# Each expert's weights read once and split in place by GpSimd, in a gated attention and mixture-of-experts block on Trainium2

## The reference

```
x = x + tanh(g_xattn) * attention(layernorm(x), keys and values from ctx and from x)   # wq, wk, wv, wo 512x512
n = layernorm(x)
shared = silu(n @ W1s.T) * (n @ W3s.T) @ W2s.T                  # 704 hidden channels
probs = softmax(n @ Wg.T); each token takes its 4 best of 16 experts, with their probs as weights
routed = sum over the 4 of  weight * (silu(n @ W1[e].T) * (n @ W3[e].T)) @ W2[e].T      # 352 hidden channels
out = x + tanh(g_ffn) * (shared + routed)
```

## Time and profile before

| what | us |
|---|---|
| timed runs, median (3 runs) | 1185.95 |
| timed runs, lowest and highest | 1185.82, 1188.97 |
| profiled execution, its own time | 1180.43 |
| its span, first to last instruction | 1178.5 |
| busy in the span: PE, PEld | 1087.8, 915.3 |
| busy in the span: DVE, ACT, POOL | 535.3, 276.4, 510.7 |
| GpSimd's subtractions of expert weights (144) | 181.6 |
| HBM read, written | 182.49 MB, 58.72 MB |

### The profile page before, as it was taken

One profiled execution on the slowest core, in us unless ns is written; L12 is line 12 of the kernel. 1 busy time (PEld: TensorE's weight loads), 2 busy tenths in 40 slices (PEclk: granted clock), 3 DMA queues, 4 the chain that ended last, 5 costly groups with the idle time before them and its releaser, 6 DMA issues. The chain is left out here.

```text
span 1178.5 us, 19426 instructions
## 1 busy us (share of the span) xinstructions
PE 1087.8 (92%) x5378; PEld 915.3 (78%) x5379; DVE 535.3 (45%) x944; ACT 276.4 (23%) x576; POOL 510.7 (43%) x632
## 2 busy tenths in 40 slices
PE   3999999999999959898979999999899999979997
PEld 3888778878878727676878888898898988967775
DVE  2243463445336257864333333334334333336846
ACT  1231132122113011111223333233233333331110
POOL 4720201202200246020666575567757775628752
PEclk9999999999999969899989999999999999988998
DMA  9411320311211446147978889887898999866775
GB/s 343 192 72 72 129 87 3 139 71 71 107 71 34 189 155 224 45 153 223 341 266 273 306 293 317 279 285 272 319 311 286 322 313 316 274 188 220 241 240 158
DMA packets 109825, 241.68 MB, mean 205 GB/s; under 512 B 13216, under 2 KB 52128, under 8 KB 101600
## 3 DMA queue, kind: packets, MB, share of 16 engines
q0 software_dynamic: 21504, 123.48, 29.6%
q1 hardware_dynamic: 77920, 98.89, 25.1%
q10 hardware_dynamic: 10368, 18.88, 4.4%
HBM read 182.49 MB, written 58.72 MB: 205 GB/s over the span
## 5 line engine op out<-in xcount | busy, mean ns | idle before, releaser
L989 POOL TENSOR_TENSOR expert_lo<-expert_raw,expert_hi (+1 forms) x144 | 181.6, 1295 | 54.5 <-DMA expert_raw<-we_rest 42.7
L88 PE MATMUL c_ps_u<-expert_hi,xT_hi 128*128 x576 | 193.1, 335 | 4.0 <-DVE xT_lo L1520 4.0
L88 PE MATMUL c_ps_u<-expert_hi,xT_lo 128*128 x576 | 186.4, 324 | 0.0
L88 PE MATMUL c_ps_u<-expert_lo,xT_hi 128*128 x576 | 185.8, 322 | 0.0
L88 PE MATMUL c_ps_y<-expert_hi,hT_hi 128*128 (+1 forms) x216 | 88.8, 411 | 29.1 <-DVE hT_lo L1525 29.1
L88 PEld LDWEIGHTS c_ps_u<-expert_hi,xT_hi 128*128 128x128 f32 x576 | 109.0, 189 | 5.6 <-issue 4.6
L88 PEld LDWEIGHTS c_ps_u<-expert_lo,xT_hi 128*128 128x128 f32 x576 | 109.6, 190 | 0.0
L88 PEld LDWEIGHTS c_ps_u<-expert_hi,xT_lo 128*128 128x128 f32 x576 | 109.0, 189 | 0.0
L1515 DVE STREAM_TRANSPOSE xT<-xs 128x512 f32<-128x512 f32 x73 | 51.5, 706 | 88.9 <-DMA xs<-bounce_dram 87.2
L88 PE MATMUL c_ps_y<-expert_hi,hT_lo 128*128 (+1 forms) x216 | 88.1, 408 | 0.0
L88 PE MATMUL c_ps_y<-expert_lo,hT_hi 128*128 (+1 forms) x216 | 88.0, 407 | 0.0
(11 more groups left out here) (263 smaller groups left out, 2356.7 us busy)
## 6 DMA issues: line engine op xcount, KB each, us to landing
expert_hi<-we POOLq DMA_DIRECT2D x16, 1920.0 KB, 8.1
expert_raw<-we POOLq DMA_DIRECT2D x14, 1920.0 KB, 13.1
xs<-bounce_dram SPq DMA_DIRECT2D x304, 64.0 KB, 2.3
y_dram<-y ACTq DMA_DIRECT2D x72, 256.0 KB, 3.9
bounce_dram<-xg SPq DMA_DIRECT2D x72, 256.0 KB, 2.8
ctxT_hi<-ctxT POOLq DMA_DIRECT2D x4, 1024.0 KB, 7.5
ctxT_raw<-ctxT SPq DMA_DIRECT2D x4, 1024.0 KB, 5.7
ctx_raw<-ctx SPq DMA_DIRECT2D x4, 1024.0 KB, 4.9
```

The costliest lines, as they stand in the source:

```text
L88: last = pe.matmul(out, a[i], b[j], start=(n == 0), stop=(n == 3 * len(pairs) - 1))
L989: last = eng.tensor_tensor(lo, raw, hi, ALU.subtract)
```

## The change

GpSimd's loads of the high part go away everywhere (expert 0, expert 1, and in each round). Each expert is loaded once, raw. `split_expert` first copies the raw weights into `w_hi`, in nine pieces of up to 512 columns, so that the copy rounds them to float32r; it waits for its own last copy on a semaphore (`hi_made`), runs a small instruction (`hold`), and then makes the nine subtractions as before, in place. The load of expert 1's raw part moves from SyncE, ahead of the stores of the sums, to GpSimd, behind a wait for all eight stores of gathered tiles. The wait for `second_raw_in` ahead of GpSimd's first step goes, since `w_in` counts that load now. The way of the tiles through DRAM stays.

```diff
-def split_expert(eng, later, base, sem, width=W13 + W2):
+def split_expert(nc, keep, eng, later, base, expert, sem):
 
-    pieces = [(P, at, min(width, W13 + W2 - at)) for at in range(0, W13 + W2, width)]
-    for rows, start, n in pieces + [(FT, W13 + W2, D)]:
+    made = keep["hi_made"]
+    pieces = [(P, at, min(D, W13 + W2 - at)) for at in range(0, W13 + W2, D)] + [(FT, W13 + W2, D)]
+    for rows, start, n in pieces:
+        hi, raw = (part(w, rows, base, start, n) for w in (later.w_hi, later.w_raw))
+        last = eng.tensor_copy(hi, raw)
+    last.then_inc(made, 1)
+    eng.wait_ge(made, expert + 1)
+    hold(nc, eng, keep, 6)
+    for rows, start, n in pieces:
         hi, lo, raw = (part(w, rows, base, start, n) for w in (later.w_hi, later.w_lo, later.w_raw))
         last = eng.tensor_tensor(lo, raw, hi, ALU.subtract)
     last.then_inc(sem, 1)
...
@@ routing_phase, SyncE
-            for v in range(QUAD):
-                sp.wait_ge(keep["bounced"][v], 32)
-            load_expert(sp, later.w_raw, WE, io, 1, keep["second_raw_in"])
...
@@ routing_phase, GpSimd
-            load_expert(pool, later.w_hi, 0, io, 0, hi_in["first"])
             pool.wait_ge(hi_in["down"], 32)
             pool.wait_ge(raw_in["down"], 32)
             split_down(pool, later.d_hi, later.d_lo, later.d_raw, True, down_ready)
-            pool.wait_ge(hi_in["first"], 32)
             pool.wait_ge(raw_in["first"], 32)
-            split_expert(pool, later, 0, first_ready, D)
+            split_expert(nc, keep, pool, later, 0, 0, first_ready)
...
             pool.wait_ge(sh.t_free, 2 * IT)
             pool.wait_ge(scheduled, 1)
-            load_expert(pool, later.w_hi, WE, io, 1, keep["w_in"])
+            for v in range(QUAD):
+                pool.wait_ge(keep["bounced"][v], 32)
+            load_expert(pool, later.w_raw, WE, io, 1, keep["w_in"])
...
@@ expert_phase, GpSimd
-                load_expert(pool, later.w_hi, base, io, e, w_in)
                 load_expert(pool, later.w_raw, base, io, e, w_in)
...
-                    pool.wait_ge(w_in, e * 64 + 32)
-                    split_expert(pool, later, base, w_ready, D)
+                    pool.wait_ge(w_in, e * 32 + 32)
+                    split_expert(nc, keep, pool, later, base, e + 1, w_ready)
...
-            pool.wait_ge(keep["second_raw_in"], 32)
```

More of the change, by code:

```diff
@@ L1057, in routing_phase @@
         raw_in = {k: sem(k + "_raw_in") for k in ("down", "first")}
-        hi_in = {k: sem(k + "_hi_in") for k in ("down", "first")}
+        hi_in = {"down": sem("down_hi_in")}
         down_ready = sem("down_ready")
@@ L1724, in program @@
         keep["y_out"], keep["base_out"] = [sem(f"y_out{v}") for v in range(QUAD)], [sem(f"base_out{u}") for u in range(2)]
-        keep["w_in"], keep["second_raw_in"] = sem("w_in"), sem("second_raw_in")
+        keep["w_in"], keep["hi_made"] = sem("w_in"), sem("hi_made")
         keep["last_down_in"], keep["last_xs_in"] = sem("last_down_in"), [sem(f"last_xs{i}_in") for i in range(IT)]
```

## The result

| what | before | after |
|---|---|---|
| timed runs, median, us | 1185.88 | 1228.47 |
| timed runs, lowest and highest, us | 1180.12, 1188.97 | 1227.21, 1233.23 |
| span of the profiled execution, us | 1178.5 | 1226.2 |
| HBM read, MB | 182.49 | 147.88 |

The ratio is 1.0372, with a 95% interval of 1.0324 to 1.0421. The change makes the kernel 3.7% slower. The forecast was 1178.3, in a range of 1168 to 1206, so both the sign and the range were wrong.

What follows compares the result with a forecast made beforehand. The prediction took GpSimd's round for each expert to set the expert stage's pace. Start -5.0, five-tile rounds -6.0, four-tile rounds -2.4 and end +5.75 summed to -7.7 us: 1178.3 against a median of 1185.95, range 1168 to 1206.

Steps and rivals of the forecast that it cites:

- Copies, hold and wait: In each split on GpSimd: nine copies 5.4 us, small held instruction 0.2, wait some 0.1, together 5.75 a round.
- The cast's slope: GpSimd's one-input cast, 0.857 ns a column, used to price a copy of 512 columns at 0.63 us.
- The rival of a dearer copy: Copies above 0.69 us make GpSimd's round longer; about 0.77 gives 1196 (chance 0.16), dearer still or no shorter queue 0.12.
- The shorter queue: GpSimd's load queue without high-part loads: first gather stored 9.7 us after the split's end, not 16.2, so 6.5 less.
- It doesn't do what it says: Rival: bytes don't hold the first gather, its wait stays near 16, rounds grow 5.75: 1267 us; within a shared 0.12.
- Raw weights: In four-tile rounds the raw weights land about 9.4 us after the split's end, ending GpSimd's wait of 6.28.
- Rounds: GpSimd's rounds: eight five-tile ones -0.75 us each to 33, six four-tile ones about -0.4 each to 26.3.
- Start and end: First split at 562.3, 5 us earlier; after the last split nothing leaves the queue, so its copies add 5.75.
- Added: nine copies ahead of the subtractions: Step pricing the new copies, hold and wait in each GpSimd split at 5.75 us, bounds 4.8 to 11.4.
- a copy of 1.03 us: Case of the dearer copy at twice the affine select's time for 256 columns: 51 us more, 1229.

Runs made afterwards that it cites:

- The moved kernel after: The changed kernel with 120 already fulfilled waits ahead of GpSimd's expert loop, which move the loop to 510 to 808 in the list: 1173.18 us, ratio 0.9913.
- 569 to 915: The moved kernel after with the nine copies, a wait and a hold made a second time in each split: 1313.02 us, ratio 1.1096.
- 580 to 878: The changed kernel with 260 already fulfilled waits ahead of GpSimd's loop instead of 120, the same work otherwise: 1233.9 us, ratio 1.0441.

## Why the prediction was wrong

The moved kernel after is the change without the refetching, and the sum can be read against it. It ran at 8.2 us below before (forecast 7.7 below, 1178.3 in all; measured 1173.18 beside 1181.34). That the two numbers lie so near is partly luck: in the two profiled executions, from which the terms below are read, the span is 4.2 shorter (1174.3 against 1178.5), and the terms come to that.

- *Copies, hold and wait.* Forecast 0.63 a copy and 5.75 a round. In the moved kernel nine copies took 5.34 in some rounds and 4.87 in the others, that is 0.63 or 0.57 for each of 8.5 widths; from the first copy to the first subtraction it was 5.57 (664.46 to 670.03) and 5.09 (691.08 to 696.17). A whole split grew from 11.4 to 17.0 in the mean of the fifteen, 5.6. Made twice the copies cost 5.7 to 5.8. The cast's slope was the right row. The rival of a dearer copy, the Trainium skill's body of 768 ns ("GPSIMD Engine Reference", section 3.1) among it, didn't come.
- *The shorter queue.* Forecast 6.5 less, a store 9.7 after the split's end. Measured 10.2 in the moved kernel, 10.4 in after: 6.0 less, the lower of the two values (6.0 and 7.1) between which 6.5 was taken. "It doesn't do what it says" is out.
- *Raw weights.* Forecast in at 9.4. In the moved kernel the load is issued at 681.77 and the next split starts at 691.08, still 1.40 idle for `we_rest`:

```profile
681.77 0.60 POOL L980 DMA_DIRECT2D expert_raw<-we  x1
...
691.08 1.18 POOL L990 CAST expert_hi<-expert_raw  x2 [1.40 <-DMA expert_raw<-we_rest]
```

  That is 9.3 after the issue. The wait of some 6 us is gone, down to the register work that I had put at 1.3.
- *Rounds.* Forecast 33.0 and 26.3; measured 33.5 in the mean of five-tile rounds, with 36.0 for the first and 33.1 for the other seven, and 26.6 for four-tile ones. From the first split to the last it is 427.7, against 431.6: -4.0, where I had -8.4. The mis-sized terms are the queue (6.0, not 6.5) and the first round, which I had at -0.75 like the others and which grew by 2.1 (567.27 to 601.15 before): there GpSimd stands 1.86 and 2.26 for "issue" where it first comes to the loop's code (0.24 and 1.00 before).
- *Start and end.* First split forecast 562.3, measured 562.21 (5.1 earlier). Last split at 989.86 against 998.88, 9.0 earlier, and the span 4.2 shorter, so the end lost 4.8 (forecast 5.75).

**The step that failed** is in "Added: nine copies ahead of the subtractions", and in the rivals. It costs an added instruction by its duration alone, and so puts the fetching of GpSimd's code at nothing without giving a reason. The change also adds 20 instructions to GpSimd's loop of four tiles, and 29 ahead of it (421 to 450 where it starts, 278 to 298 in length). By that the loop came to lie over four pieces of code, and at each of the 16 jumps back between its 17 passes (the first four tiles are written out ahead of it) GpSimd fetched code again: 80 packets more, five for each jump. DMA traffic of the kernel after between 654 and 1070 us, in which it jumps back 14 times:

```profile
q14 instruction: 70, 0.57, 0.4%
```

The moved kernel has one packet in the same stretch. The fetching costs 55.3 us (1228.47 less 1173.18; 50.8 when each is set against before on its own chip), seven times the net gain that I had added up. None of my rivals had it: 1229 stands in the text, but for a copy of 1.03 us, so the number is there by chance and its mechanism isn't.

Why one fetch costs what it does is not shown. After ten of the 16 jumps back the stall at the column copy lasted 4.9 to 8.0 us. After the other six there was none there, since the first packets had come during a split, and one of 2.8 to 3.7 followed two gathers later. The two packets in the stall of 5.73 have 1.0% of the DMA engines' time, 0.9 us of one engine, so most of the stall isn't their own transfer. Nor is the weights' share what sets its length: it was 78% there, but 20% in the stall of 6.55 that ends at 734.02 and 44% in the one of 7.39 that ends at 768.86. With all queues together the engines were 79% busy or more in these three. Whether the fetch would be quicker on idle engines wasn't tried.

The stall delays the gathers, then SyncE's stores and loads of `xs`, then VectorE, in whose order the next turn stands ahead of the low half of `h`, and so TensorE. At its longest:

```profile
1083.56 0.79 PE L88 MATMUL c_ps_y<-expert_hi,hT_hi 128*128 x1 [13.05 <-DVE hT_lo L1527]
```

During and behind that stand TensorE's granted clock was 0.50 (1076 to 1084 us) and 0.55 (to 1088), the lower of its two levels (1.2 GHz), and a matmul took 0.63 us where it takes 0.39 to 0.40 at the upper one (2.4 GHz), which it had again from 1088. From the first split to the last the granted clock was 0.94, in the moved kernel 0.99. So a part of the loss is slower matmuls: they are busy 1099.1 us in all, against 1087.8 before.

All waits at the column copy, for "issue" and for stored rows, come to 109.2 us in the kernel after (99.4 and 9.8) and to 51.0 in the moved one (1.9 and 49.1). That is 58.2 more, near the 51 to 55 that reach the end.

The Trainium skill has the mechanism. "Advanced Engine Details and Errata", section ISA Cache, gives 32 KB in two lines of 16 KB (256 instructions), and "Runtime: NRT & Kernel Launch", section Instruction fetch mechanics, says that a taken branch to code outside the two pages held forces a fetch before execution goes on. The runs agree that a jump back can cost a fetch. They differ on the size: by two lines of 256 the loops at 569 to 915 and at 580 to 878 would need no fetch, and they had 97 and 96 packets. Three pieces of 128 agree with all. A jump back brought five packets where the loop touches four pieces, so one more than it touches. That would fit four pieces held, one of them fetched ahead, which is the 32 KB of the page; no run was made to tell this apart from three held.

## What to carry to other kernels

Before an instruction is added to an engine's loop, find where the loop lies in that engine's compiled list, and count the instruction packets on the page before and after: if they rise from a constant few to several for each pass, the time has little to do with what was added. A comparison of two versions that differ in code length is only fair when both loops lie inside the pieces that are kept; moving one with a few idle instructions, run once, is a cheap control. Where two engines block each other, cut the long one's work into pieces that the other has the slack to wait for: here wide one-input copies won 14 us, and wide two-input subtractions lost it again.

## What the runs showed of the hardware

- A loop of GpSimd over three pieces of 128 instructions ran without fetching code in each pass. Over four there were 95 to 97 packets of the instruction queue instead of 14 to 18, five for each of 16 jumps back, and the kernel took 34 to 61 us more.
- 120 waits that are already fulfilled make 60 instructions in the list (and 60 more in the profile, 19572 against 19512).
- A copy on GpSimd that rounds float32 to float32r takes 0.57 to 0.63 us for 128x512 (nine in 4.87 or 5.34); a subtraction about 1.31 (nine in 11.13). The wider copies are cheaper by the column: 67.2 us against 82.5 for all experts.
- A GpSimd subtraction of 8.3 us stretched a two-input instruction of VectorE from 0.68 to 8.76. The Trainium skill ("SBUF — State Buffer", section Terms) says that VectorE and GpSimd lock a shared port pair for a whole instruction and that the loser waits; the number agrees. With copies of 3840 columns and subtractions of 512 the longest was 3.78, and with copies of at most 2048 and subtractions of 1024 it was 2.60, at the same time within the intervals.
